# Decoder layer on one core: the first three FFN units with x1 transposed inside the unit, and the down product split by feature chunk

## The reference, cut to what matters

```python
x = layernorm(x + attn(x))                        # "x1"
x = layernorm(x + (x + xattn(x, ctx)) ...)        # "x2": xattn quantises x1 and ctx to fp8 with one scale each
...
mlp = silu(x @ gate_w) * (x @ up_w) @ down_w      # 512 -> 2048 -> 512
# experts: queries = x @ W_q, routing over product keys, top 8 of 1024 rows gathered from down_embed and up_embed
x = layernorm(x + mlp + experts)
```

## Time and profile before

| | us |
|---|---|
| median of 3 runs | 844.67 (841.53 to 845.09) |
| profiled execution | 843.72 |
| its span | 841.9 |
| unit 0, from its first matmul to unit 1's | 27.14 |
| unit 1 | 26.98 |
| unit 2, to unit 3's first matmul, with the query product | 37.09 |

### The profile page before, as it was taken

The page is one execution under the profiler, slowest core; times in us unless marked ns, Lnnn a source line. Parts: engine busy times, 40 slices in busy tenths (PEclk is TensorE's granted clock), DMA queues, the critical chain, the costliest instruction groups (busy, mean ns, idle before and its releaser), DMA issues. The chain is left out here.

```text
span 841.9 us, 10386 instructions
## 1 busy us (share of the span) xinstructions
PE 780.5 (93%) x3506; PEld 634.1 (75%) x3510; DVE 686.4 (82%) x1329; ACT 296.9 (35%) x657; POOL 369.0 (44%) x296
## 2 busy tenths in 40 slices
PE   4999899999749888999999999999999999999994
PEld 3877788877526675888888888888877877887783
DVE  5687588778889776156769999999999999999997
ACT  4352435343053342213253333433333333333320
POOL 0232121214213221103357866775667776766431
PEclk9999999998969999999999999999999999999998
DMA  9557513595315552100112232322233333232113
GB/s 327 198 112 181 100 59 100 115 285 100 50 65 125 126 125 82 43 1 1 59 47 63 74 107 60 91 74 72 89 110 91 89 90 104 72 86 69 38 72 129
DMA packets 51047, 81.69 MB, mean 97 GB/s; under 512 B 17488, under 2 KB 26448, under 8 KB 50481
## 3 DMA queue, kind: packets, MB, share of 16 engines
q0 software_dynamic: 24384, 33.48, 18.6%
q1 hardware_dynamic: 25024, 47.52, 16.2%
q10 hardware_dynamic: 1584, 0.01, 0.1%
HBM read 110.44 MB, written 12.58 MB: 146 GB/s over the span
## 5 line engine op out<-in xcount | busy, mean ns | idle before, releaser
L1495 PE MATMUL gu<-x_hi,w_hi 128*128 128x512 f32 x528 | 207.0, 392 | 5.3 <-DVE x_lo L1282 3.3
L1496 PE MATMUL gu<-x_lo,w_hi 128*128 128x512 f32 x528 | 205.5, 389 | 0.0
L1497 PE MATMUL gu<-x_hi,w_lo 128*128 128x512 f32 x528 | 205.5, 389 | 0.0
L1054 POOL TENSOR_TENSOR h_lo<-mid,h_hi 128x512 fp32r<-128x512 f32 x62 | 79.4, 1302 | 110.5 <-ACT h_hi L1165 110.0
L1495 PEld LDWEIGHTS gu<-x_hi,w_hi 128*128 128x128 f32 x528 | 99.1, 188 | 28.8 <-DVE mid L1288 4.6
L1497 PEld LDWEIGHTS gu<-x_hi,w_lo 128*128 128x128 f32 x528 | 99.1, 188 | 20.7
L1496 PEld LDWEIGHTS gu<-x_lo,w_hi 128*128 128x128 f32 x528 | 99.1, 188 | 20.4
L1175 ACT ACTIVATE gates<-dots 128x1 f32<-128x1 f32 x144 | 29.2, 203 | 232.8 <-DVE dots L1379 229.5
L1068 POOL DMA_INDIRECT ctx_q<-table_dram,row_i x64 | 80.7, 1261 | 62.4 <-DVE xall L1388 40.6
L1068 POOL DMA_INDIRECT scratch<-table_dram,row_i x64 | 83.0, 1297 | 39.4 <-issue 21.3
L1495 PE MATMUL ob<-w_hi,h_hi 128*128 128x512 f32 x248 | 97.4, 393 | 1.0 <-POOL h_lo L1054 1.0
(11 more groups left out here) (195 smaller groups left out, 1373.4 us busy)
## 6 DMA issues: line engine op xcount, KB each, us to landing
stage<-in_ctx SPq DMA_DIRECT2D x7, 1024.0 KB, 5.5
total<-prod POOLq DMA_DIRECT2D x12, 512.0 KB, 4.7
xall<-half_bo POOLq DMA_DIRECT2D x4, 1024.0 KB, 9.9
xhat<-in_L_ffn_gate_w SPq DMA_DIRECT2D x8, 512.0 KB
xhat<-in_L_ffn_up_w SPq DMA_DIRECT2D x8, 512.0 KB
xall<-in_mask_Bx1xS_ff POOLq DMA_DIRECT2D x4, 1024.0 KB, 13.5
xhat<-in_L_ffn_down_w SPq DMA_DIRECT2D x8, 512.0 KB
x_dram<-xall SPq DMA_DIRECT2D x4, 1024.0 KB, 6.8
```

The source lines that it names most:

```text
L1054: nc.gpsimd.tensor_tensor(lo[:, c], mid[c][:], hi[:, c].bitcast(F32), ALU.subtract).then_inc(hlo_done, 1)
L1495: nc.tensor.matmul(dst, lhs[0], rhs[0], start=start, stop=False)
L1496: nc.tensor.matmul(dst, lhs[0], rhs[1], start=False, stop=False)
L1497: return nc.tensor.matmul(dst, lhs[1], rhs[0], start=False, stop=stop)
```

## The change

In units 0, 1 and 2:

- x1 of batch n + 2 is transposed inside unit n, through banks `gu[0]` and `gu[1]` only: tiles 0 and 1 after the cross product, tiles 2 and 3 between gate and up of chunk 1. ACT's `scaled` follows in two pairs around the second `silu`.
- The down product of unit n follows in unit n, chunk by chunk (`down_early`): chunk 0 behind up of chunk 1, then x2 of batch n + 1 transposed, then chunk 1. `down(2)` behind the query goes.
- POOL issues the mask DMA of batch n + 2 ahead of the power step of batch n + 1; each batch has a semaphore of its own for it.
- DVE normalises ahead of the second `middle`, and takes quantise and accumulate in smaller turns.
- The first query product no longer waits for all of x2_lo.

```diff
+            def x1t_bank(b, i):
+                return i if b < 2 else i % 2
...
                     low_h(n, 0)
+                    if n + 2 < TB:
+                        add_mask(n + 2)
                     if n + 1 < TB:
                         power(n + 1)
                     low_h(n, 1)
-                    if n + 2 < TB:
-                        add_mask(n + 2)
...
                     unit(n, 0)
-                    unit(n, 1)
                     if n + 2 < TB:
-                        scaled(n + 2)
+                        scaled(n + 2, (0, 1))
+                    silu(n, 1)
+                    if n + 2 < TB:
+                        scaled(n + 2, (2, 3))
+                    high_h(n, 1)
+                    if n + 2 < TB:
                         high_w(load_index(1, n), 1, 1, n, load_index(1, n) % 2)
...
-                middle(0, 0)
-                residual(1, range(TB))
-                variance(v3_ready)
-                middle(0, 1)
-                normalise(1, r3_ready, x2_done)
-                for n in range(1, TB - 1):
-                    low_x2(n)
-                    quantise(n + 1, (0, 1))
-                    accumulate(n - 1, n - 1, True)
-                    quantise(n + 1, (2, 3))
+                for n in range(TB - 1):
                     middle(n, 0)
                     residual(n + 1, range(TB))
                     variance(v3_ready)
+                    if n + 2 < TB:
+                        quantise(n + 2, (0,))
+                    normalise(n + 1, r3_ready, x2_done)
                     middle(n, 1)
-                    normalise(n + 1, r3_ready, x2_done)
+                    if n + 2 < TB:
+                        quantise(n + 2, (1,))
+                        low_x2(n + 1)
+                        accumulate(n, n, True, (0, 1))
+                        quantise(n + 2, (2,))
+                        accumulate(n, n, True, (2, 3))
+                        quantise(n + 2, (3,))
...
+                def down_early(n, c, free):
+                    pe.wait_ge(hlo_done, GC * n + c + 1)
+                    if n == 0 and c == 0:
+                        pe.wait_ge(wlo_done, 3)
+                    for i in range(TB):
+                        free(i)
+                        ts = slice(i * P, (i + 1) * P)
+                        last = three(ob[i][:], [h[:, c, ts] for h in h_of(n)], [w[:, c] for w in down_s[0]], c == 0, c == GC - 1)
+                        if c == GC - 1:
+                            last.then_inc(down_mm, 1)
...
+                def x2_bank_free(n):
+                    def free(i):
+                        if i >= 2:
+                            pe.wait_ge(mid_done, GC * n + 2)
+                        elif n + 2 < TB:
+                            pe.wait_ge(y_done, TB * (n + 2) + 3 + i)
+                        else:
+                            pe.wait_ge(mid_done, GC * n + 1)
+                    return free
...
                 for n in range(TB - 1):
-                    transposes(n, x2t_mm, freed(y_done, TB * (n + 1)), x2_done)
-                    if n:
-                        down(n - 1, 0, 3 if n == 1 else None, freed(z2_done, TB * n))
                     pe.wait_ge(l2_done, TB * (n + 1))
                     gate_up(n, 0, n, 0, 2 if n == 0 else None)
                     cross(n + 1, freed(acc_done, TB * (n - 1)) if n else freed(z2_done, 0))
-                    gate_up(n, 0, n, 1, None)
                     if n + 2 < TB:
-                        transposes(n + 2, x1t_mm, freed_pair(mid_done, GC * n))
-                transposes(3, x2t_mm, freed_pair(mid_done, 2 * GC), x2_done)
+                        transposes(n + 2, (0, 1), x1_bank(n + 2), x1t_mm, first_half_free(n))
+                        gate_up(n, 0, n, 1, None, lambda: transposes(n + 2, (2, 3), x1_bank(n + 2), x1t_mm, freed(y_done, TB * (n + 2) - 2)))
+                    else:
+                        gate_up(n, 0, n, 1, None)
+                    down_early(n, 0, freed(z2_done, TB * (n + 1)))
+                    transposes(n + 1, range(TB), own_bank, x2t_mm, x2_bank_free(n), x2_done)
+                    down_early(n, 1, nothing)
...
                     pe.wait_ge(l2_done, 3 * TB + b + 1)
-                    if b == 0:
-                        pe.wait_ge(l2_done, 4 * TB)
...
-                down(2, 0, None, freed(z2_done, 3 * TB))
```

More of the change, by code:

```diff
@@ L145, in decoder_layer @@
         w_in_s = [sem("w_in0"), sem("w_in1")]
-        whi_done, wlo_done, xm_in = sem("whi_done"), sem("wlo_done"), sem("xm_in")
+        whi_done, wlo_done, xm_in = sem("whi_done"), sem("wlo_done"), [sem(f"xm_in{b}") for b in range(B)]
         def add_mask(b):
@@ L1136, in high_w, with scaled @@
                     nc.scalar.activation(flat(hi, r), stage_of(r, slot), ACT.Copy).then_inc(whi_done, 1)
-                def scaled(b):
-                    for i in range(TB):
+                def scaled(b, tiles):
+                    for i in tiles:
                         j = TB * b + i
@@ L1144, in scaled @@
                             act.wait_ge(q_done, j - TB + 1)
-                        nc.scalar.activation(y_q[i], gu[i][:], ACT.Copy, scale=scale_x[:, 0:1]).then_inc(y_scaled, 1)
+                        nc.scalar.activation(y_q[i], gu[x1t_bank(b, i)][:], ACT.Copy, scale=scale_x[:, 0:1]).then_inc(y_scaled, 1)
                         act.wait_ge(y_scaled, j + 1)
@@ L1177, in experts @@
                         nc.scalar.activation(coef[:, t % 2, k:k + 1], gates[:, t % 2, k:k + 1], ACT.Copy, scale=prob[:, t, k:k + 1]).then_inc(coef_done, 1)
-                scaled(0)
-                scaled(1)
+                scaled(0, range(TB))
+                scaled(1, range(TB))
                 high_w(2, 0, 0, 2, 0)
@@ L1288, in middle, with accumulate @@
                     nc.vector.tensor_tensor(mid[c][:], gu[2 * c + 1][:], mid[c][:], ALU.mult).then_inc(mid_done, 1)
-                def accumulate(n, tb, first=False):
+                def accumulate(n, tb, first=False, tiles=range(TB)):
                     if first:
@@ L1497, in three, with transposes @@
                     return nc.tensor.matmul(dst, lhs[1], rhs[0], start=False, stop=stop)
-                def transposes(b, count, free, ready=None):
-                    for i in range(TB):
+                def transposes(b, tiles, bank, count, free, ready=None):
+                    for i in tiles:
                         free(i)
@@ L1506, in transposes @@
                             j = TB * b + i
-                            last = nc.tensor.transpose(gu[i][:, c * P:(c + 1) * P], xall[:, j * D + c * P:j * D + (c + 1) * P], ident[:])
+                            last = nc.tensor.transpose(gu[bank(i)][:, c * P:(c + 1) * P], xall[:, j * D + c * P:j * D + (c + 1) * P], ident[:])
                         last.then_inc(count, 1)
@@ L1516, in cross, with gate_up @@
                         last.then_inc(cross_mm, 1)
-                def gate_up(n, g_set, tb, c, w_loads):
+                def gate_up(n, g_set, tb, c, w_loads, between=None):
                     cols = slice(tb * S, (tb + 1) * S)
@@ L1526, in gate_up @@
                     last.then_inc(gate_mm, 1)
+                    if between is not None:
+                        between()
                     if w_loads is not None:
@@ L1543, in down, with own_bank, x1_bank, first_half_free @@
                         last.then_inc(down_mm, 1)
+                def down_early(n, c, free):
[8 more added lines that the diff above has]
+                            last.then_inc(down_mm, 1)
                 def freed(count, base):
                     return lambda i: pe.wait_ge(count, base + i + 1)
[L1548 to L1550 removed]
                 def nothing(i):
                     pass
+                def own_bank(i):
+                    return i
+                def x1_bank(b):
+                    return lambda i: x1t_bank(b, i)
+                def first_half_free(n):
+                    return lambda i: pe.wait_ge(mid_done, GC * n + 1)
+                def x2_bank_free(n):
[7 more added lines that the diff above has]
+                    return free
                 cross(0, nothing)
[L1556 removed]
+                transposes(1, range(TB), own_bank, x1t_mm, freed(y_done, 0))
+                transposes(0, range(TB), own_bank, x2t_mm, freed(y_done, TB), x2_done)
                 for n in range(TB - 1):
[L1558 to L1560 removed]
                     pe.wait_ge(l2_done, TB * (n + 1))
```

4 lines of the change are left out of this document (2 added, 2 removed).

## The result

| | us |
|---|---|
| changed kernel, median of 5 runs | 834.74 (830.53 to 835.45) |
| before, median of 5 runs on the same chip | 845.09 (841.53 to 845.72) |
| ratio, 95% interval | 0.9874 (0.9843 to 0.9906) |
| forecast | 833.8 (830 to 839) |

The change saves 10.4 us by the medians; the forecast was 10.9.

The account below looks back on a forecast made before the run. PE, busy 93% of the span, was taken to bound the kernel. Savings of 3.3 + 3.2 + 4.4 = 10.9 us bring the profiled 843.72 to 832.8, and with the median 0.95 higher 833.8; range 830.0 to 839.0.

Parts of the forecast that it names:

- PE full behind the stage: PE stays full from 331.44 through the expert units, so time taken from its path before 348 comes off the end.
- Rival C: Expert units keep a pace not tied to unit 3's start, so the end does not move: 844; chance 0.09.
- PE's own work, 23.34 us a unit: PE's matmuls and transposes in unit 0 or 1 of the new order, without waits, sum to 23.34 us.
- (1): In units 0 and 1, x1's second pair reuses banks 0 and 1; its wait for ACT is covered by about 0.5 us.
- rival E: A stall in the middle of gate/up replaces the one removed: saving 7.9, 836.8; chance 0.06.
- (2): x2's transposes no longer meet ACT: x1's second pair is read by about 16.0 us, PE returns at 18.8.
- (3): Mask DMA, power, normalise, mid, h_hi, h_lo: the second down chunk waits 0.4 us, so a unit takes 23.75 us.
- Rival A: DVE's quantise holds up GpSimd's h_lo in units 0 and 1, costing 2 x 0.6 = 1.2 us: 835.0; chance 0.12.
- Power behind the DMA: GpSimd's power step follows the mask DMA's issue of 1.31 us and takes 1.02, ending 15.9 us into the unit.
- B: Slow power step, 3.00 us against 1.02, costs 4.0 of the saving in units 0 and 1: 837.8; chance 0.06.
- Unit 2, 4.4 us less: Unit 2 with the four query products takes 32.7 us instead of 37.09, 4.4 us less.
- The sum: Savings of units 0, 1 and 2 together: 3.3 + 3.2 + 4.4 = 10.9 us.

Follow-up runs that it names:

- the experiment: Changed kernel with DVE's quantise of the second tile moved behind low_x2: 831.62 us in one run, unit 1 at 23.76 us.
- the split alone: Changed kernel with x1's transposes put back behind the unit's matmuls, ACT and POOL in their former orders, down product still split: 834.95 us, ratio 0.9888.
- power first: Changed kernel with POOL's power step ahead of the mask DMA in units 0 and 1: 834.24 us in one run.
- the mask last: Changed kernel with the power step first and the mask DMA back behind the second h_lo on POOL: 831.41 us in one run.
- x1 only: Kernel before with x1's transposes moved inside the unit, ACT's scaled in two pairs, no first-query wait for all x2_lo: 854.27 us in one run.
- x1 only, weight late: As x1 only, but with the weight's high part behind the x2_hi copies on ACT: 843.06 us in one run.

## Why the prediction was right, step by step

- **PE full behind the stage.** Right: 493.87 us after unit 3's start against 494.02. Rival C is out.
- **PE's own work, 23.34 us a unit.** Right: 23.40 with every wait gone. The offsets in unit 1 of the changed kernel: first x1 pair at 8.90 (8.72 in the sum), gate 9.70 (9.58), second pair 12.55 (12.40), down 16.16 (16.08), x2 18.88 (18.80).
- **(1) x1's second pair covered by 0.5 us.** Right, no wait there in any trace; rival E is out.
- **(2) x2's transposes no longer meet ACT, and x2_lo is just in time.** Right: PE waits for neither in the changed kernel.
- **(3) The longest chain.** The mechanism was right, place by place: the mask DMA starts 13.89 us into unit 1 (13.5 forecast; 0.31 pass between the transposes' end at 291.75 and the issue), power ends at 16.28 (15.9), normalise takes 1.92 (2.05), mid starts at 18.15, h_hi at 18.87, h_lo at 19.58. Up to there the chain was about as forecast. h_lo was **the term that was mis-sized**: 1.72, not 1.29, so that the second chunk started at 21.35 and not at 20.95. The step in the text that failed is "I take from this that DVE alone pays". The row behind it (h_lo 1.29 us from 272.92) was read against a line that merges four tiles of normalise. The single tile under way then had 0.16 us left, so h_lo had hardly anything to wait for and the row couldn't tell the two rules apart. Another row of the trace of before did show POOL paying: a weight's low part, released with 0.50 us of quantise's first operation left, took 2.76 us and not 2.40 as at 278.83. In the changed kernel h_lo comes with 0.58 left and takes 0.43 longer; the experiment took away the neighbour and with it the cost. From the trace of before, DVE and POOL:

```profile
272.54 0.54 DVE L1276 TENSOR_SCALAR xall<-xall,mv,rstd 128x512 f32<-128x512 f32 x1
```

```profile
256.53 0.68 DVE L1247 SCALAR_TENSOR_TENSOR scratch<-scratch 128x512 f32<-128x512 bf16 x1
```

```profile
256.71 2.76 POOL L1049 TENSOR_TENSOR w_lo<-xhat,w_hi 128x1024 fp32r<-128x1024 f32 x1 [4.19 <-DVE x_lo L1282]
...
278.83 2.40 POOL L1049 TENSOR_TENSOR w_lo<-xhat,w_hi 128x1024 fp32r<-128x1024 f32 x1 [3.37 <-ACT w_hi L1136]
```

- **Rival A** had a chance of 0.12 and a price of 0.6 a unit. It is what happened, at 0.44 a unit. The measured 834.74 is 0.3 us from its sum (835.0) and 0.9 from the main one (833.8), but runs that spread over 5 us can't choose between the two; the rows of h_lo do.
- **Power behind the DMA.** Off by 0.5: 1.58 us instead of 1.02. It starts 0.81 us behind the issue's start and not 1.31, so the two together took 2.39 us where the sum had 2.33: here two errors cancel, which is luck. B's 3.00 did not come.
- **Unit 2, 4.4 us less.** Measured: 37.09 against 21.58 + 10.88 = 32.46, so 4.6. The wait of 0.35 for h_lo didn't show: h_lo ended at 320.79, PE came at 321.13.
- **The sum.** 3.3 + 3.2 + 4.4 = 10.9 forecast, 2.78 + 2.78 + 4.63 = 10.19 in the traces, 10.4 in the medians.

What the forecast didn't say, and the runs do, is how unevenly the parts carry it. ACT's waits were 3.6 us a unit in the trace of before. Taking them away alone made the kernel slower, and with the weight out of the way it was worth about 0.7 a unit; the split alone kept 8 of 10.

## What to carry to other kernels

Where a producer chain through three engines ends in front of the matmul engine, look for matmul work of about the chain's slack that is ready earlier, and put it in between, cutting a product by its contraction chunks if need be. Taking away the wait that shows in the trace is worth little until the next one behind it is covered as well, and an engine that comes free earlier may start work (here a weight's low part on GpSimd) that blocks another one on the path. Time each half of a change that has two.

## What the runs showed of the hardware

- GpSimd's tensor operation on 128x512 took 1.71 to 1.72 us when it came 0.11 us behind the start of a DVE operation with two SBUF inputs, 1.27 to 1.29 with that neighbour moved away. The Trainium skill, SBUF — State Buffer, "SBUF: two separate sides", says that where such a DVE operation starts first, GpSimd's blocks until it is done. The trace agrees in direction; the row grew by 0.43 where DVE's operation had about 0.58 left.
- How much a GpSimd row grew went with what the DVE operation had left at its start, less about 0.15 us: 0.43 with 0.58 left (h_lo), 0.39 with 0.52 (power in the kernel with power first), 0.36 with 0.50 (a weight's low part before), 0.02 with 0.16 (h_lo before). Beside DVE's x2_lo, which reads one of its two inputs from PSUM, the weight's low part took 2.40 us and didn't grow.
- The other direction costs more, since GpSimd's operations are long: four normalise tiles took 1.92 us alone, 3.12 beside h_lo, 4.92 and 6.05 beside h_lo and a weight's low part.
- A power step of four columns took 1.02 us alone, 1.41 with quantise beside it and 1.55 to 1.58 behind a DMA issue. A weight's low part behind a DMA issue took 2.92 and 2.95 us with the mask last, 2.40 otherwise: about 0.5 more too.
- In two of the kernels the granted clock fell behind a row of waits on PE. A down product of 24 matmuls took 8.13 and 7.32 us behind waits of 1.40, 0.79 and 3.0 (x1 only), and 6.82 us behind 1.40 and 0.78 (x1 only, weight late, unit 1), instead of 5.7; waits of 1.40 and 0.79 in unit 0 of that second kernel left it at 5.7. A wait can so cost more than its own length, and not in each place.
